# Mixing stage: the recurrence's two products from GpSimd to VectorE, with the order of a bank read, of a sum into x and of the prologue changed

## The reference

```
k, v, r = mix(xn, time_mix_k) @ w_key, mix(xn, time_mix_v) @ w_value, mix(xn, time_mix_r) @ w_recept
# mix(y, m) = y*m + shifted(y)*(1-m); per channel, along the tokens:
out   = (e1 * alpha + e2 * v) / (e1 * beta + e2)
alpha = d1 * alpha + d2 * v
beta  = d1 * beta + d2
x     = x + (out * sigmoid(r)) @ w_output
xn2   = layer_norm(x)
vk    = square(relu(mix(xn2, f_time_mix_k) @ f_w_key)) @ f_w_value
x     = x + sigmoid(mix(xn2, f_time_mix_r) @ f_w_recept) * vk
```

## Time and profile before

| what | us |
|---|---|
| median of 3 runs | 1583.56 (1581.69 to 1587.66) |
| the profiled execution, its time | 1581.56 |
| its span | 1579.8 |
| PE busy in the span | 1362.9 (86%) |
| DVE busy | 924.3 (59%) |
| POOL busy | 680.1 (43%) |

### The profile page before, as it was taken

One profiled execution on the slowest core, in us unless ns is written; L12 is line 12 of the kernel. 1 busy time (PEld: TensorE's weight loads), 2 busy tenths in 40 slices (PEclk: granted clock), 3 DMA queues, 4 the chain that ended last, 5 costly groups with the idle time before them and its releaser, 6 DMA issues. The chain is left out here.

```text
span 1579.8 us, 27682 instructions
## 1 busy us (share of the span) xinstructions
PE 1362.9 (86%) x7400; PEld 1108.9 (70%) x7401; DVE 924.3 (59%) x2098; ACT 666.1 (42%) x1497; POOL 680.1 (43%) x616
## 2 busy tenths in 40 slices
PE   4999975899999999336999999998937899999996
PEld 3998974778888888313665666576636788888885
DVE  5778776444444444277789888886145344444443
ACT  3576753222323333244557656764332223333332
POOL 3666743244445555213324323422132344455553
PEclk9899995899999999767999999999957999999998
DMA  6476662855553333420000000000017755533332
GB/s 207 182 245 230 214 250 82 281 136 132 128 134 54 58 57 54 128 82 1 1 14 28 14 13 27 27 14 27 14 41 229 236 131 130 134 54 60 54 54 37
DMA packets 100874, 157.84 MB, mean 100 GB/s; under 512 B 10256, under 2 KB 60688, under 8 KB 100816
## 3 DMA queue, kind: packets, MB, share of 16 engines
q1 hardware_dynamic: 73120, 118.67, 21.6%
q0 software_dynamic: 27264, 37.82, 14.5%
q10 hardware_dynamic: 432, 0.66, 0.2%
HBM read 95.89 MB, written 61.21 MB: 99 GB/s over the span
## 5 line engine op out<-in xcount | busy, mean ns | idle before, releaser
L1081 DVE TENSOR_TENSOR second_hT_lo<-bank,second_hT_hi 128x512 fp32r<-128x512 f32 x71 | 49.1, 692 | 170.3 <-ACT second_hT_hi L963 161.3
L1832 PE MATMUL bank<-b_xfk,b_fk 128*128 128x512 f32 x256 | 122.6, 637 | 27.1 <-DVE b_xfk L1595 16.7
L1081 DVE TENSOR_TENSOR first_hT_lo<-bank,first_hT_hi 128x512 fp32r<-128x512 f32 x71 | 49.1, 692 | 165.3 <-ACT first_hT_hi L963 156.3
L929 POOL DMA_INDIRECT out_x<-second_block_hot,second_add_token x53 | 84.0, 1585 | 127.6 <-DMA out_x<-second_block_hot,second_add_token 67.1
L929 POOL DMA_INDIRECT x_rows<-first_block_hot,first_add_token x53 | 84.0, 1584 | 125.8 <-DMA x_rows<-first_block_hot,first_add_token 67.9
L155 PE MATMUL bank<-second_ring,second_xT_hi 128*128 x284 | 120.8, 425 | 9.5 <-issue 7.4
L155 PE MATMUL bank<-first_ring,first_xT_hi 128*128 x284 | 120.5, 424 | 2.2 <-DVE first_xT_lo L1069 2.2
L1832 PEld LDWEIGHTS bank<-b_xfk,b_fk 128*128 128x128 f32 x256 | 51.3, 204 | 94.5 <-issue 64.8
L1753 PE MATMUL bank<-b_fv,b_hT 128*128 128x256 f32 x512 | 114.6, 383 | 0.0
L156 PE MATMUL bank<-first_ring,first_xT_hi 128*128 x284 | 113.5, 400 | 0.0
L157 PE MATMUL bank<-second_ring,second_xT_lo 128*128 x284 | 113.4, 399 | 0.0
(11 more groups left out here) (352 smaller groups left out, 3930.9 us busy)
## 6 DMA issues: line engine op xcount, KB each, us to landing
first_ring<-split_weights SPq DMA_DIRECT2D x96, 256.0 KB
second_ring<-split_weights SPq DMA_DIRECT2D x96, 256.0 KB
a_wraw<-in_L_ffn_w SPq DMA_DIRECT2D x24, 512.0 KB, 6.6
split_weights<-a_whi SPq DMA_DIRECT2D x24, 512.0 KB, 2.7
split_weights<-a_wlo SPq DMA_DIRECT2D x24, 512.0 KB, 4.1
normed_rows<-xg SPq DMA_DIRECT2D x16, 528.0 KB, 3.0
x_rows<-x SPq DMA_DIRECT2D x8, 512.0 KB, 7.2
x<-x_rows SPq DMA_DIRECT2D x8, 512.0 KB, 9.0
```

The lines of the kernel that those rows point to most:

```text
L929: nc.gpsimd.indirect_dma_start(x_dram[:], bass.IndirectOffsetOnAxis(ap=add_token[q][:], axis=0), y[q], None, compute_op=ALU.add).then_inc( ...
L1081: nc.vector.tensor_tensor(hT_lo[par][:].rearrange("p k t -> p (k t)"), th_bank[par][:], hT_hi[par][:].rearrange("p k t -> p (k t)").bitcas ...
L1832: last = nc.tensor.matmul(xb_[m % 4][:], fk_s[:, i, m * P:(m + 1) * P], xfk[:, i, :], start=(i == 0), stop=(i == KC - 1))
```

## The change

Both products go to DVE: `dv` into a function of its own behind the channel mix, `num` behind the scan `be`. `finish(b-1, 1)`, the read of the value product's bank, then comes before the scan instead of behind `denominator`. On ACT `weights_of_step` is cut in two, the relus (`gaps_of_step`) before `xn2T` and the exponentials behind it, and `carry(b+1)` moves from ahead of `hidden(b)` to behind the receptance and the gate's norm. On POOL `add_mixed(b)` moves behind the gate's norm of b-1 and waits for a new semaphore `num_ready`, which DVE raises right ahead of the reciprocal. In the prologue the transposes of `xn`(1) and their reading come before the projections of sequence 0, and each of `mix_time`'s three outputs waits only for the projection that read its tile last.

```
@@ scalar
-            def weights_of_step(b):
+            def gaps_of_step(b):
                 act.wait_ge(gam_ready, b + 1)
                 nc.scalar.activation(d1[:], gam[:], ACT.Relu).then_inc(expd, 1)
                 nc.scalar.activation(d2[:], gam[:], ACT.Relu, scale=-1.0).then_inc(expd, 1)
+
+            def weights_of_step(b):
                 act.wait_ge(expd, 6 * b + 1)
...
+            evacuate_xn(1)
             evacuate_k(0)
             evacuate_v(0)
-            evacuate_xn(1)
+            gaps_of_step(0)
...
                     evacuate_v(b + 1)
-                    weights_of_step(b + 1)
+                    gaps_of_step(b + 1)
                 evacuate_xn2(b)
                 if has_next(b, 1):
+                    weights_of_step(b + 1)
                     evacuate_r(b + 1)
...
-                if has_next(b, 1):
-                    carry(b + 1)
                 hidden(b)
...
                     route_norm(b - 1)
+                if has_next(b, 1):
+                    carry(b + 1)
@@ gpsimd
-            def decayed_value(b):
-                wait_apart(pool, kvr_evac, 6 * b + 4, passed["pool"])
-                wait_apart(pool, expd, 6 * b + 4, passed["pool"])
-                nc.gpsimd.tensor_tensor(dv[:], d2[:], v[:], ALU.mult).then_inc(dv_ready, 1)
-
-            def first_value(b):
-                wait_apart(pool, expd, 6 * b + 6, passed["pool"])
-                nc.gpsimd.tensor_tensor(num[:], rho[:], v[:], ALU.mult).then_inc(num_begun, 1)
...
                 rstd(mv2, shift2, own_2, var2_ready, rstd2_ready, b)
-                add_mixed(b)
                 if has_next(b, 2):
                     rstd_in(b + 2)
-                if has_next(b, 1):
-                    decayed_value(b + 1)
-                if has_next(b, 1):
-                    first_value(b + 1)
                 if has_before(b, 1):
                     add_channel(b - 1, 1)
                     rstd(mvg, shiftg, own_c, varg_ready, rstdg_ready, b - 1)
+                if has_next(b, 1):
+                    wait_apart(pool, num_ready, b + 2, passed["pool"])
+                add_mixed(b)
                 add_channel(b, 0)
@@ vector
+                    if src is xnT:
+                        wait_count(dve, kvr_done, 6 * b - 4 + 2 * n)
...
-                wait_count(dve, kvr_done, 6 * b)
...
+            def decayed_value(b):
+                r_.round(b)
+                dve.wait_ge(kvr_evac, 6 * b + 4)
+                dve.wait_ge(expd, 6 * b + 4)
+                r_.link(nc.vector.tensor_tensor(dv[:], d2[:], v[:], ALU.mult))
...
+                dve.wait_ge(expd, 6 * b + 6)
+                nc.vector.tensor_tensor(num[:], rho[:], v[:], ALU.mult)
                 r_.link(last)
...
+                dve.sem_inc(num_ready, 1)
                 r_.link(nc.vector.reciprocal(den[:], den[:]))
...
                 mix_channel(b)
                 if has_next(b, 1):
-                    denominator(b + 1)
+                    decayed_value(b + 1)
                 if has_before(b, 1):
                     finish(b - 1, 1)
                 if has_next(b, 1):
+                    denominator(b + 1)
                     numerator(b + 1)
@@ tensor
             transposes(xn, 0)
+            pe.wait_ge(xn_ready, 2)
+            transposes(xn, 1)
             project_k(0)
             project_v(0)
-            pe.wait_ge(xn_ready, 2)
-            transposes(xn, 1)
             project_r(0)
```

More of the change, by code:

```diff
@@ L1245, in phase_mix @@
                                                           sem("expd"))
-        dv_ready, num_begun, g_ready = sem("dv_ready"), sem("num_begun"), sem("g_ready")
+        num_ready, g_ready = sem("num_ready"), sem("g_ready")
         wo_done, xb_ready, xn2_ready, mix2_ready = sem("wo_done"), sem("xb_ready"), sem("xn2_ready"), sem("mix2_ready")
@@ L1486, in period @@
                     route_norm(b - 1)
+                if has_next(b, 1):
+                    carry(b + 1)
+                if has_before(b, 1):
                     gate_rows(b - 1)
@@ L1549, in _ @@
             rstd_in(1)
-            decayed_value(0)
-            first_value(0)
             def period(b):
                 rstd(mv2, shift2, own_2, var2_ready, rstd2_ready, b)
-                add_mixed(b)
                 if has_next(b, 2):
                     rstd_in(b + 2)
-                if has_next(b, 1):
-                    decayed_value(b + 1)
-                if has_next(b, 1):
-                    first_value(b + 1)
                 if has_before(b, 1):
@@ L1573, in _ @@
             f, m_, m2, e_, r_, w_, g_, s_ = (OwnSteps(dve, sm, n) for sm, n in (
-                (own_f, 1), (own_m, 1), (own_m2, 1), (own_e, 1), (own_r, 4), (own_w, 1), (own_g, 1), (own_s, 1)))
+                (own_f, 1), (own_m, 1), (own_m2, 1), (own_e, 1), (own_r, 6), (own_w, 1), (own_g, 1), (own_s, 1)))
             def statistics(src, bnt, mvt, own, done):
@@ L1592, in mixes @@
                 own.link(nc.vector.tensor_tensor(dT[:], src[:, :, 1:N + 1], src[:, :, 0:N], ALU.subtract))
-                for dst, m in outs:
+                for n, (dst, m) in enumerate(outs):
+                    if src is xnT:
+                        wait_count(dve, kvr_done, 6 * b - 4 + 2 * n)
                     for i in range(KC):
@@ L1625, in exponents @@
                 last.then_inc(del_ready, 1)
+            def decayed_value(b):
[3 more added lines that the diff above has]
+                r_.link(nc.vector.tensor_tensor(dv[:], d2[:], v[:], ALU.mult))
             def denominator(b):
-                r_.round(b)
-                dve.wait_ge(expd, 6 * b + 4)
                 for i in range(KC):
                     last = nc.vector.tensor_tensor_scan(be[:, i, 1:N + 1], d1[:, i, :], d2[:, i, :], 0.0, ALU.mult, ALU.add)
+                dve.wait_ge(expd, 6 * b + 6)
+                nc.vector.tensor_tensor(num[:], rho[:], v[:], ALU.mult)
                 r_.link(last)
-                dve.wait_ge(expd, 6 * b + 6)
                 nc.vector.tensor_tensor(den[:], rho[:], be[:, :, 0:N], ALU.add)
             def numerator(b):
-                dve.wait_ge(dv_ready, b + 1)
                 for i in range(KC):
@@ L1642, in numerator @@
                 r_.link(last)
-                dve.wait_ge(num_begun, b + 1)
                 r_.link(nc.vector.tensor_tensor(num[:], num[:], al[:, :, 0:N], ALU.add))
@@ L1648, in quotient @@
                 dve.wait_ge(kvr_evac, 6 * b + 6)
-                nc.vector.scalar_tensor_tensor(out=num[:], in0=sg[:], scalar=1.0, in1=num[:], op0=ALU.add, op1=ALU.mult)
+                r_.link(nc.vector.scalar_tensor_tensor(out=num[:], in0=sg[:], scalar=1.0, in1=num[:], op0=ALU.add, op1=ALU.mult))
+                dve.sem_inc(num_ready, 1)
                 r_.link(nc.vector.reciprocal(den[:], den[:]))
@@ L1701, in _ @@
             mix_time(1)
+            decayed_value(0)
             denominator(0)
```

## The result

The changed kernel takes 1544.45 us (median of 4 runs, 1543.41 to 1545.24); beside it the kernel before took 1582.62. The ratio is 0.9756, interval 0.9728 to 0.9784: 38 us faster. I had predicted 1551 with a range of 1545 to 1562: the direction and the mechanism held, and the gain was larger than forecast by 6.5 us, 0.55 beyond the range's edge. The profiled execution took 1545.24 with a span of 1543.5.

A forecast was written before the change was run, and what follows sets the result against it. PE, carrying 86% of the span, was taken as the bound, with waits for DVE's xfk and fs and slow clock behind gaps. Gains 3.6 + 4.6 + 6.4 + 13.2 + 2.7 + 1.8 = 32.3 us gave 1551, range 1545 to 1562.

The forecast's parts named there:

- Both gaps close: 2.69 a period: Loop periods, channel mix: PE's idle 0.56 and 2.13 us, before chunks 0 and 3, both vanish.
- With no gap I take the slow stretch to go too: Periods 2 to 4: the slow-clock matmuls behind the gap return to full clock, another 1.70 us each.
- Rival A: The clock falls even without the gaps: 3 x 1.70 and 2.65 stay, gain 24.5 us, time 1559; chance 0.15.
- Prologue, "1.2 later": project_k(0), now behind the transposes of xn(1), starts 1.2 us later (0 to 2); prologue net gain taken as 3.6.
- Period 0, "I count 1.2 against it": Period 0: slow clock behind PE's shortened wait costs 1.2 us more, leaving 4.6 of the 5.8 taken off.
- The wait of 4.9: Period 0: PE's wait before the channel mix, 10.70 us before, shrinks by 5.8 and leaves 4.9 idle.
- The base: Starting time for the 32.3 us gain: profiled 1581.56 gives 1549.3, median 1583.56 gives 1551.3; 1551 predicted.
- Costed at nothing: Added DVE products before gT, the later add_mixed and carry chain, and the sum under the reciprocal: covered by about 5 us, cost 0.
- B: A new wait in each period, sg or fs late, PE waiting a us in seven periods: gain 21, time 1562; chance 0.15.
- C: Slower: chain num_ready, add_mixed, carry, time_output is 10.8 us late; 1592 or more; chance 0.03.
- D: DVE stays as late because products replace the stalls; only period 0 or prologue gains: about 1577 to 1583; chance 0.04.
- the waits at the start of the stage: PE's waits at the mixing stage's start, called the same in both kernels because the chain between engines is unchanged.

The follow-up runs named there:

- a1: Kernel before with only both products moved to DVE (dv behind the channel mix, num behind the scan be); ratio 0.9856 to before.
- a2: Kernel before with only finish(b-1, 1), the bank's read, put directly behind the channel mix; ratio 0.9897 to before.
- c1: Changed kernel with xv and xr of sequence 1 made behind quotient(0) in the prologue; 1544.69 us, ratio 0.9761.
- b2: Changed kernel with finish(b-1, 1), the bank's read, behind the denominator again; 1545.49 us, ratio 0.9779.
- b3: Changed kernel with add_mixed(b) back right behind the second norm's steps, without the num_ready wait, carry staying moved; 1544.19 us, ratio 0.9776.
- b4: Changed kernel with the old prologue order on PE and ACT, mix_time's separate waits kept; 1544.91 us, ratio 0.9784.
- b1: Changed kernel with both products back on POOL; 1544.67 us, ratio 0.9794.
- a5: Kernel before with only the ACT order changed: relus ahead of xn2T, exponentials behind it, products still on POOL; ratio 0.9876 to before.
- a4: Kernel before with only the new prologue order and mix_time's three separate waits; ratio 0.9984 to before.
- a6: Kernel before with two parts: both products on DVE and finish(b-1, 1) between dv and the scan; ratio 0.9806 to before.
- a3: Kernel before with only the sum into x moved behind the gate's norm, under the reciprocal, and carry behind that norm on ACT; ratio 0.9952.

## Why the prediction came out as it did

The step that failed is a size, spread over three terms: the idle time of the gaps, the prologue and period 0 (2.8, 0.9 and 1.1 us too small). The mechanism held.

- **"Both gaps close: 2.69 a period", period "49.7"**: they closed, and the period became 49.17. The 0.56 and 2.13 are reckoned from modelled ends of matmuls, and each gap hid 0.26 more, as a1 and a2 measure. That is 0.5 in each of periods 2 to 5 and 0.3 in 6. Period 1, with one gap, gained 0.4 more than reckoned: its 32 matmuls take 13.90 at full clock, not the 14.16 scaled up from 20, and in the unbroken stream they start 0.16 before the row of the value product ends. In all that is 2.8 us of the miss.
- **"With no gap I take the slow stretch to go too"**: right. The granted clock is 1.00 over the loop period. Rival A is out: in no kernel here did the clock fall in the loop without a gap. The two measured short ones, 0.92 and 0.57 as shown, didn't bring it down.
- **Prologue, "1.2 later"**: the start of `project_k(0)` did come 1.05 later. But the eight matmuls took 4.25 us instead of 6.29, since the granted clock, 0.50 in the transposes of `xn`(1) ahead of them, was 1.00 from 681 on, early in the projection; in c1, behind the same transposes, it was still 0.50 at 683. `rho` came about 1.0 earlier instead of 1.2 later. The other parts were as reckoned (3.19, 4.3 and 2.45), so `gT(0)` came 6.0 earlier, not 3.6. Against that `wo` took 6.71 instead of 5.15, at the slow clock for longer: net 4.5 at `project_k(1)`. How early the clock rises in `project_k(0)` is in part luck, as the fourteen times above show. The net isn't: b2 and b3, with a slower projection and a faster `wo`, come to `project_k(1)` after 58.8 and 58.4, the changed kernel after 58.5. For the order alone b4 gives 0.4 to 0.8 us there (59.2).
- **Period 0, "I count 1.2 against it"**: not charged in this profile (15.67 for the 32 matmuls, 15.60 before), nor in those of b1 and c1 behind the same wait, but charged in those of b2, b3, b4 and a5 (16.8 to 17.0). It is luck of the execution, not a term. The wait of 4.9 was right (4.97), but it is for `sg`; the prediction said only that `r` must be read at about the same time.
- **The base**: 1551 was 32.3 below the median of 1583.56, which lay 2.0 above the profiled execution. The changed kernel's profiled execution took 1545.24, 0.8 above its median. The stage gave 5.0 more than reckoned, the rest of the span 1.0 less; with the 2.0 and 0.8 that is the distance from 1551.3 to 1544.45. Which part of the 2.8 is real can't be told: medians of the kernel before went from 1578 to 1583 between the sets of runs.
- **"Costed at nothing"**: right in all three. `gT` ended at 902.65, where PE wanted it at 907.3; `carry` ended at 904.3, where `time_output` began at 909.2; the sum ran inside the reciprocal. The rule of the Trainium skill (SBUF — State Buffer, "Who interferes with whom"), that a DVE instruction with one SBUF input doesn't hold GpSimd, holds here for 128x1024 too: 2.36 us beside a reciprocal of 6.55.
- **Rivals B, C, D** did not occur. What the prediction left out, without its costing anything, is what each part is worth: it priced places in the timeline and not the four parts. Alone they add up to half as much again as the whole (56 against 37, a1 to a4), and with three of them in place the fourth is worth 0.4 to 3.1 us of stage, of which up to 1.5 is the clock (b1 to b4). Two of them alone, the products and the bank's read, give 30.7 of the 37.3 (a6).
- **A sentence that doesn't hold**: the prediction calls the waits at the start of the stage the same in both kernels, and then shortens one of them in its prologue term. The term is right: PE's wait for `gT` went from 25.80 to 21.62.

The range's low edge, 6 below the forecast, was too near: it held my own 2 us for the prologue and period 0 but nothing for the gaps, though all of these errors go the same way, towards more gain.

## What to carry to other kernels

Where two engines block each other, ask whose instruction the stall falls on, and who waits for that one: here, with the same two products on GpSimd, a loop period was 4.9 us longer than the changed kernel's where they fell on `xfk` and `xfr` (before; 1.7 of it slow clock), 2.0 where they fell on `be` and the denominator (a5), and no longer where they fell on `xfr` alone (b1, which also reads the bank early). Parts of a change that each give cover to one chain need not add up; after measuring the whole, take each out once, and keep the ones that are simple. For the size of a gap, compare two periods, one with it and one without, instead of taking the idle time as shown.

## What the runs showed of the hardware that I had not expected

- A break in a stream of matmuls costs about 0.26 us beyond the idle time in the rows: 0.92 shown cost 1.19, 0.57 cost 0.82, and 1.70 cost 51.13 - 49.17 = 1.96.
- The moment at which the granted clock rises varies between executions of the same order: the eight matmuls of `project_k(0)` took 4.21 to 5.76 us behind the same transposes, in seven kernels. Behind a gap of 2.13 us the clock fell in some periods of an execution and not in others (three of four in the kernel before, two of four in a4), behind one of about 2.5 in one of four (a3), and behind 1.70 in none of four (a5).
- A whole 128x1024 sum on GpSimd fits under a VectorE reciprocal of the same size at no cost to either, 2.36 and 6.55 us. Beside the scan `eps` the same sum held VectorE for 1.7 (2.90 against 1.23), and a product of that size beside the pair of `xfk` for 2.1 (3.51 against 1.42).
